# Both halves of the experts' input on VectorE, and a width-one tail moved by one group

## The reference

```python
def _layernorm(x, axis=-1, eps=1e-05):
    m = jnp.mean(x, axis=axis, keepdims=True)
    v = jnp.var(x, axis=axis, keepdims=True)
    return (x - m) / jnp.sqrt(v + eps)

# L0_xattn: 16 heads of width 16 over 77 context rows, the best 32 kept
scores = jnp.einsum('bhsd,bhnd->bhsn', Q, K) / SCALE
topk_scores, topk_indices = jax.lax.top_k(scores, k)
sparse_weights = jax.nn.softmax(topk_scores, axis=-1)
context = jnp.einsum('bhsk,bhskd->bhsd', sparse_weights, sel_V)
return context @ Wo.T + bo
...
# L0_ffn: the best 2 of 8 routed experts, and shared experts
logits = xf @ router_w + router_b
topk_vals, topk_idx = jax.lax.top_k(logits, BEST_K)
gates = jax.nn.softmax(sparse, axis=-1)
routed_out = jnp.einsum('etd,te->td', routed, gates)
return (routed_out + shared_out).reshape(B, S, D)
...
# L2_attn: 64 heads of width 1, causal
dots = jnp.einsum('bhid,bhjd->bhij', q, k) * scale
dots = jnp.where(causal, dots, -jnp.inf)
attn = jax.nn.softmax(dots, axis=-1)
out = jnp.einsum('bhij,bhjd->bhid', attn, v)
return jnp.einsum('bnh,ch->bnc', out, w_out)
```

## Time and profile before

| | |
|---|---|
| median of 3 runs | 3096.11 us (3092.39 to 3096.82) |
| the profiled execution | 3093.96 us |
| its span, first to last instruction | 3092.2 us |
| mean granted clock of TensorE | 0.971 |
| busy TensorE / VectorE / ScalarE / GpSimd | 92% / 60% / 40% / 16% of the span |

### The profile page before, as it was taken

How to read it: one execution, slowest core, us unless ns; L and a number is a source line. 1 busy time by engine, 2 the same in 40 slices (tenths; PEclk the granted TensorE clock), 3 DMA queues, 4 the chain that set the end, 5 groups by cost and what they waited for, 6 DMA issues and landing times.

```text
span 3092.2 us, 52038 instructions
## 1 busy us (share of the span) xinstructions
PE 2857.2 (92%) x20501; PEld 1897.8 (61%) x20533; DVE 1852.9 (60%) x6428; ACT 1241.4 (40%) x1933; POOL 494.0 (16%) x554
## 2 busy tenths in 40 slices
PE   7999999998999889987998889899999999998998
PEld 4666666875565556655555445566766676676653
DVE  5543433689999536775787887663334434435455
ACT  1222221335656433323443689444322333323443
POOL 0010010113444221002120368200000000000000
PEclk9999999999999999998999899999999999998999
DMA  3000000010000100000000111100000000000000
GB/s 132 1 1 0 1 1 1 1 39 16 1 1 2 35 33 1 1 1 6 2 2 1 23 42 29 42 1 28 1 1 1 1 0 1 0 1 9 2 1 28
DMA packets 22028, 37.74 MB, mean 12 GB/s; under 512 B 2132, under 2 KB 19733, under 8 KB 20760
## 3 DMA queue, kind: packets, MB, share of 16 engines
q1 hardware_dynamic: 20968, 34.02, 3.3%
q10 hardware_dynamic: 816, 0.39, 0.1%
HBM read 26.81 MB, written 2.10 MB: 9 GB/s over the span
## 4 chain that ended last, share of the span: by engine, by line
PE 72%; DVE 19%; ACT 5%; issue 3%; POOL 0%; DMA 0%; SPq 0%; DVEq 0%; ACTq 0%; POOLq 0%
PE ps L416 44%; DVE arena L571 3%; PE ps L623 3%; ACT arena L679 2%; PE ps L3317 2%; PE ps L3336 2%; PE ps L695 2%; DVE arena L2141 2%; PE ps L519 1%; PE ps L754 1%; PE ps L1805 1%; DVE arena L2134 1%; PE ps L3190 1%; PE ps L556 1%; ACT arena L2562 1%
## 5 line engine op out<-in xcount | busy, mean ns | idle before, releaser
L416 PE MATMUL ps<-weights,arena 128*128 128x256 f32 (+4 forms) x2480 | 691.9, 428 | 18.1 <-ACT arena L1954 5.5
L416 PEld LDWEIGHTS ps<-weights,arena 128*128 128x128 f32 (+1 forms) x2480 | 463.2, 196 | 177.4 <-issue 97.9
L416 PE MATMUL ps<-arena,weights 128*128 128x256 f32 (+4 forms) x1662 | 543.5, 475 | 13.6 <-DMA weights<-in_w_L_attn 5.9
L416 PEld LDWEIGHTS ps<-arena,weights 128*128 128x128 f32 (+1 forms) x1662 | 304.2, 191 | 215.3 <-issue 155.3
L416 PE MATMUL ps<-arena 128*128 128x256 f32 (+4 forms) x1618 | 425.7, 416 | 10.6 <-issue 4.6
L416 PEld LDWEIGHTS ps<-arena 128*128 128x128 f32 (+2 forms) x1618 | 298.0, 188 | 119.2 <-issue 79.4
L571 DVE TENSOR_REDUCE arena<-ps 128x16 f32<-128x1232 f32 (+2 forms) x96 | 179.1, 1866 | 142.6 <-PE ps L556 45.8
L679 ACT ACTIVATE arena<-ps 77x2048 f32<-77x2048 f32 (+1 forms) x112 | 210.1, 1876 | 116.5 <-PE ps L623 59.2
L2141 DVE MATCH_REPLACE8 arena<-arena 128x77 f32<-128x77 f32 x1024 | 213.9, 224 | 0.0
L915 POOL TENSOR_TENSOR x<-x,weights 128x512 f32<-128x512 f32 x32 | 44.9, 1402 | 988.7 <-DVE arena L881 943.4
L2562 ACT ACTIVATE arena<-ps 128x1536 f32<-128x1536 f32 x128 | 178.3, 1466 | 28.3 <-PE ps L2551 28.0
(11 more groups left out here) (440 smaller groups left out, 4409.9 us busy)
## 6 DMA issues: line engine op xcount, KB each, us to landing
arena<-arena SPq DMA_DIRECT2D x156, 32.0 KB
weights<-in_w_L_ffn SPq DMA_DIRECT2D x1, 3848.0 KB, 11.5
weights<-in_w_L_attn SPq DMA_DIRECT2D x1, 3840.0 KB, 15.2
weights<-in_w_L_xattn SPq DMA_DIRECT2D x3, 1024.0 KB, 6.3
weights<-in_w_L_ffn SPq DMA_DIRECT2D x1, 3072.0 KB, 10.6
x<-in_x SPq DMA_DIRECT2D x2, 1024.0 KB
weights<-in_w_L_xattn SPq DMA_DIRECT2D x1, 2048.0 KB, 7.4
out<-x SPq DMA_DIRECT2D x8, 256.0 KB, 2.2
```

The source lines that it names most:

```text
L416: ins = k.nc.tensor.matmul(out, lhsT, rhs, start=start and i == 0, stop=i == n - 1)
```

## The change

In selected attention VectorE makes both halves of z, with a `hold` ahead of them, in `expert_batch_z_vector`; GpSimd makes none and so doesn't wait for the norm steps any more. In the width-one stage the sums are turned back one group later (11 for 10), the means turned and copied one group later (14 for 13), and the output product is moved from group 15 to the start of the next window, but for the last window. The fp8 products and their wait move by a group, VectorE's `fp8_scaled_vector` from group 14 to 15, and its `fp8_shifted_vector` from (3, 15) to (4, 0).

```diff
-def expert_half_z_vector(k, dve, s, u):
+def expert_batch_z_vector(k, dve, s, u):
     experts(dve, s, u, "norm", 13)
-    k.nc.vector.tensor_scalar(s.f.z[:, 0, :], k.xs[:, SPARE + 2 * u.n, :], s.f.mv[:, 0, 0:1], s.f.rstd[:, 0:1],
-                              ALU.subtract, ALU.mult).then_inc(*s.sig.up("f_z"))
+    hold(k, dve, "vector")
+    for t in (0, 1):
+        k.nc.vector.tensor_scalar(s.f.z[:, t, :], k.xs[:, SPARE + 2 * u.n + t, :], s.f.mv[:, t, 0:1],
+                                  s.f.rstd[:, t:t + 1], ALU.subtract, ALU.mult).then_inc(*s.sig.up("f_z"))
...
     if last and at == Z_AT:
-        expert_half_z_vector(k, dve, s, last)
+        expert_batch_z_vector(k, dve, s, last)
...
-def expert_z_gpsimd(k, pool, s, u):
-    experts(pool, s, u, "norm", 13)
-    hold(k, pool, "gpsimd")
-    k.nc.gpsimd.tensor_scalar(s.f.z[:, 1, :], k.xs[:, SPARE + 2 * u.n + 1, :], s.f.mv[:, 1, 0:1], s.f.rstd[:, 1:2],
-                              ALU.subtract, ALU.mult).then_inc(*s.sig.up("f_z"))
...
     for n in range(B + 2):
         now, last, older, soon, later = neighbours(s.steps, n)
-        if last:
-            expert_z_gpsimd(k, pool, s, last)
         if older:
...
# L2_attn_tensor
-            if n in (1, 3) and g == 14:
+            if n in (1, 3) and g == 15:
                 pe.wait_ge(*s.sig.at("oT", 0, last, 1))
                 fp8_products_tensor(k, pe, x, x.steps[n // 2 - 2], None, 6)
-            if n in (1, 3) and g == 15:
-                experts(pe, x, x.steps[n // 2 - 2], "scaled")
+            if n in (2, 4) and g == 0:
+                experts(pe, x, x.steps[n // 2 - 3], "scaled")
+            if n >= 2 and g == 0:
+                means_out_tensor(k, pe, s, n - 2, tail_bank(n - 1))
...
-            if g == 10 and n:
+            if g == 11 and n:
...
                 sums_back_tensor(k, pe, s, last, tail_bank(n))
...
-            if g == 13 and n:
+            if g == 14 and n:
                 means_turn_tensor(k, pe, s, last, tail_bank(n))
-            if g == 15 and n:
+            if g == 15 and n == B:
                 means_out_tensor(k, pe, s, last, tail_bank(n))
...
# L2_attn_scalar
-            if g == 13 and n:
+            if g == 14 and n:
                 act.wait_ge(*s.sig.at("oT_ps", 0, last, 1))
...
# L2_attn_vector
-            if at in ((1, 14), (3, 14)):
+            if at in ((1, 15), (3, 15)):
                 fp8_scaled_vector(k, dve, x, older if n == 1 else left, 6)
...
-            if at in ((2, 3), (3, 15)):
+            if at in ((2, 3), (4, 0)):
                 fp8_shifted_vector(k, dve, x, older if n == 2 else left)
```

## The result

The changed kernel takes 3101.76 us (median of 10 runs, 3095.42 to 3107.59), the one before 3095.25 (median of 10, 3088.23 to 3096.82). The ratio is 1.0025 with a 95% interval of 1.0013 to 1.0036: slower by some 8 us (the medians are 6.5 apart), where I had forecast 5.5 us faster. The ten runs lie over 12 us, those of before over 9.

The account below looks back on a forecast made before the run. It took TensorE and VectorE as the bounds in selected attention, and engines waiting for one another in width-one attention. +2.2 - 7.7 = -5.5 us gave 3090.6 us against the median of 3096.11; range 3083 to 3099.

Parts of the forecast that it names:

- the price of the block: Selected attention: GpSimd's addition of the expert output (L2207) blocks VectorE's z; z 0.2 us later, VectorE's next instruction 1.2 later.
- part A: Selected attention, z on VectorE: eight windows together cost +2.2 us.
- rival 3: Selected attention: z waits for all three GpSimd additions, +2.1 us a window, +17 in all; total 3105.4 us; chance 0.12.
- The bound that I gave, +0.47: Selected attention: z's upper bound of lateness in us, both halves wholly behind GpSimd's one addition of the expert output.
- First window: Selected attention: GpSimd's two bias additions run first, z +0.5 us, with a norm step blocked by 0.1, +0.6.
- the seventh: Selected attention, seventh window: the addition of the expert output is long over when z starts, -0.6 us.
- rival 1: Selected attention: no block of z by GpSimd, so -4.0 us there, total -11.7, 3084.4 us; chance 0.15.
- Part B: Width-one stage: the tail moved by one group of four heads saves 7.7 us.
- The terms of windows 1 and 2: Width-one stage: TensorE's waits at the transposes of the sums go, -2.2 and -2.3 us.
- Windows 4 to 7: Width-one stage: ScalarE's waits for turned means and next scores shrink, -0.8, -0.8, -0.5 and -1.5 us.
- The border of windows 3 and 4: Width-one stage: the shifted fp8 block stands ahead of window 4's second product, +0.4 us, between -0.5 and +0.9.
- Rival 2: Width-one stage: late VectorE gives the tail's gain back, leaving -1.2 us; total 3097.1 us; chance 0.23.

Follow-up runs that it names:

- part A alone: The kernel before with only z moved to VectorE, the width-one stage unchanged: 3111.15 us, ratio 1.0056.
- the order experiment: Part A alone, with GpSimd's two bias additions moved behind its two tensor_scalars of the later z: 3097.0 us, ratio 1.0015 to the kernel before.
- the guard: Part A alone, with GpSimd waiting for both halves of z before it adds the expert output: 3086.1 us, ratio 0.9978 to the kernel before.
- The kernel released by the norm steps: Part A alone, with GpSimd waiting for the 13th norm step before its additions: 3097.31 us, ratio 1.0017 to the kernel before.

## Why the prediction was wrong

**The step that failed** is the price of the block: "I take the block as real and price it so: L2207 runs 764.91 to 766.00, the blocked first half ends 0.15 later, the second half 0.35 after that, z at 766.50." The block was real and fell where I said. Its length was not that of L2207 but of the three additions in a row, 3.16 us a pair in place of some 1.6. z is 1.76 us later in five windows, where I had 0.2, and VectorE's next instruction 2.8 us, where I had 1.2. The term of part A, +2.2 us, was +18.1 in the profile, and some +17 (1.0056) with part A alone. It was rival 3, to which I gave 0.12: +2.1 a window, 17 in all. Its mechanism is shown by the order experiment (1.58 with one addition ahead of one-input work, 3.16 with three) and by the guard (0.72). That its 17 us fit is luck: I priced eight windows by a lateness of 2.1. Only five have the three additions, each late by 1.75, which is 8.8; 5.9 more came in those of the five that had run at a higher clock before, where I had allowed 1.5 to 3 us either way for the clock; and the windows around them gave the other 3.4 (+1.8 up to the first z, +1.5 to the second, +0.8 between the last two, -0.7 behind).

**Why I took the wrong price.** The pair in the earlier trace rows ended 0.19 us after a second addition had begun, and I read that as a proof that VectorE gets in between. But it had started 0.16 us *before* GpSimd. The kernel released by the norm steps has both cases in one run: a lead of 0.08 for VectorE gives 1.50, a lead of 0.13 for GpSimd 3.01. The row was of the first kind. In the change the two start within 0.02 us of each other, and that was held like the second kind. I had also written that the two start "in the same 0.1 us" and not asked what each order costs. The bound that I gave, +0.47, assumed one addition; a bound for it has to take in every instruction queued behind.

**The other terms of part A.** First window: I had a norm step blocked by 0.1; it was blocked for 1.72 - 0.14 = 1.6. In the seventh I was right: the pair takes 0.72, and the turn starts 0.78 us after z's start for 1.46. In the eighth it took 10.3 us from the reciprocal to z for 9.3, +1.0 where I had +0.9. What rival 1 supposes, z without a block, is what the guard builds: I had -4.0 for it, its ratio gives about -7 and its stage -6.5.

**Part B** came out near in sum and wrong in its parts. I had -7.7; by itself the stage took 6.2 us less, in the changed kernel 4.5. The terms of windows 1 and 2, -2.2 and -2.3, failed: the move of the sums is worth nothing, +1.2 and -1.6. In window 1 I had capped them by VectorE's idle time up to the border, but that idle time lies at 1783.89 and later, after the wait, and VectorE was full up to there (0.1 us idle from 1766 on). Windows 4 to 7, -3.6 in my sum, gave about -4.9 in the intervals of the kernel without the sums' move, most of the difference in the last (-2.2 for -1.5). The border of windows 3 and 4 lost nothing that shows (-0.8 in the third interval for +0.4). Rival 2 did not happen.

**The range** of 3083 to 3099 missed 3101.76 by 3 us. Part A alone was further out, at 3111, and part B brought it back.

## What to carry to other kernels

An instruction on one engine may be of use by what it keeps waiting. Before taking one away, list what stands behind it in its queue, when each of these becomes ready, and which instruction of the shared neighbour runs at that moment. When VectorE's and GpSimd's elementwise work can start together, order them by a wait (VectorE's critical instruction first): here it has GpSimd start 0.8 us after z in place of 0.02, which nothing waits for, and takes the choice away from some hundredths of a microsecond. And idle time of an engine covers a move only if it lies where the move needs it.

## What the runs showed that I had not expected

- A tensor_scalar of 128 x 256 on VectorE (0.40 us) is held by back-to-back two-input GpSimd instructions until the last is over: pairs of 1.58, 3.01 and 3.16 us for 0.72. VectorE leading by 0.01 to 0.02 us didn't help it, by 0.08 it let the pair through after the first addition, and by 0.48 the pair was untouched. The 1.58 had one addition ahead of one-input work; the 3.01 and 3.16 are of rows of three.
- The Trainium skill ("SBUF — State Buffer", section "Who interferes with whom") says that the first to issue has the shared ports for the whole instruction and the other one blocks fully. The lead of 0.48 us agrees (0.72 us), and so does GpSimd's of 0.13 and 0.07 with one addition (1.44 and 1.49). The lead of 0.01 with its 3.16 does not follow from it by the times of the trace, nor that VectorE's waiting pair isn't let in between the additions of a row (3.01 us).
- A norm step on 128 x 2 elements was held as long as a large one: 1.72 us for 0.14.
- One-input GpSimd tensor_scalars did not hold VectorE's: the pair ended at 764.13 while one ran from 763.64. That one took 1.42 us for 1.21.
- With TensorE's clock at 0.93 to 0.94, the window followed the start of z's turn one for one: the turn 0.78, 1.46, 1.64 and 3.21 us after z's start gave 52.14, 52.83, 53.01 and 54.58 us, in four kernels.

The spread of the changed kernel's ten runs, 3095 to 3108 us, goes with TensorE's granted clock: 0.972 in the two fastest, 0.968 in the three slowest, some 3 us for a thousandth. The kernel before has as wide a spread in later measurements (33 runs, 3084.8 to 3098.1, 0.974 to 0.969). Part of it lies where no kernel differs: the first reciprocal of selected attention starts at 698.9 to 704.8 us in the fourteen profiles.

What stays open: whether the hold itself lowers the clock, and whether some executions have fewer held windows; only one execution of each kernel was profiled.
